# The graph layer's norm and linear part moved into the attention loop, and its scatters six to an iteration

## The chip, the cores and the metric

The kernel runs on one core of a Trainium2 chip. The metric is the time of one execution on the device in microseconds. Four engines compute: TensorE (PE, matrix products and transposes into PSUM banks), VectorE (DVE), ScalarE (ACT) and GpSimd (POOL). POOL also issues the indirect DMAs, whose addresses are rows of an index tensor; SyncE (SP) issues the plain ones. Engines run their own instruction streams and wait for each other on semaphores.

## The reference

Two layers act on 64 x 256 = 16384 tokens of width 64. The change lies between the local attention and the feed-forward part of layer 1. Its attention (`_L1_attn_ref`) works in windows of 64 tokens with 8 heads, and its feed-forward part is gated by a graph layer over 262144 edges:

```python
h = h + _L1_attn_ref(_layernorm(h), ...)
h = h + _L1_ffn_ref(_layernorm(h), ...)

# in _L1_ffn_ref, x = _layernorm(h), M = 16384 nodes, 4 heads x 4 experts
h = (x_flat @ W_gat).reshape(M, HEADS, NUM_EXPERTS)
a_src = (h * att_src).sum(-1)
a_dst = (h * att_dst).sum(-1)
e = leaky_relu(a_src[src] + a_dst[dst], 0.2)
e_max = segment_max(e, dst); ee = exp(e - e_max[dst])
alpha = ee / (segment_sum(ee, dst)[dst] + 1e-16)
agg = segment_sum(h[src] * alpha[:, :, None], dst) + b_gat
scores = _layernorm(agg, ln_gamma, ln_beta).reshape(M, HEADS, NUM_EXPERTS).mean(1)
topk_s, topk_i = top_k(scores, TOP_K); w = softmax(topk_s)
for ei in range(NUM_EXPERTS):
    g = where(topk_i == ei, w, 0.0).sum(-1)
    hh = gelu(x @ W1[ei] + b1[ei])
    out = out + g[..., None] * (hh @ W2[ei] + b2[ei])
```

## The kernel before

The 16384 rows are 128 tiles of 128. The residual `H` (in the rows: h_res) and the normed `xn` lie in SBUF for all tiles. The edges have been sorted by destination earlier, and while FFN0 (layer 0's experts) runs, POOL looks up for each node where its edges begin and end.

*Attention loop.* `Fori(0,AI=32)` on PE (L624) and ACT (from L828); DVE's loop is written out in Python (from L1230). An iteration handles four tiles, one in each of four lanes `AL`, with two PSUM banks per lane: `ps[0]` are banks 0, 2, 4, 6 and `ps[1]` banks 1, 3, 5, 7. The steps are listed in `A_STEPS`: PE does xT, qkv, sc, PT, pv, oT, pj; ACT does xs, xTs, q (L835), ex (L837), PTs (L838), oTs (L839), with xs being L831 and xTs L833; DVE does kb (L1238), vb (L1241), mx (L1243), sb (L1244), sm (L1245), rc (L1246), on (L1247), h (L1250). Each step is one instruction or a few for each lane, all four lanes before the next step, and `need` makes an engine wait for named steps of the others. All products go through the helper `mm` (L398), so rows of PE all have that line. Ahead of an iteration's steps DVE calls `prepare(i)`, which finishes the edge search in pieces: comparisons at i = 4 to 7, end positions at 8, operations over 128x2048 at 25 to 30, the rest at 31, where it raises `s_gi`.

*norm(2)*, L1102 to L1109 on DVE and L792 to L798 on ACT: mean, squares, deviation and product over all tiles in two halves.

*Linear part.* `Fori(0,GI=16)` with two lanes `GL` of four tiles. ACT copies `xn` (L848), PE transposes it (xT), ACT copies the transpose (L851, `xTs`), PE multiplies by `gw` (hg), ACT copies the 16 values of each node into `nodeG` (L854), DVE forms the source and destination terms (L1262 and L1263, twice). SP stores the transposes (L292, read back by ffn1) and the node rows (L294). POOL scatters the destination terms, one indirect DMA per tile, to the first edge of each node (L378).

*Gather stage.* POOL then gathers the node row of each edge's source, 32 chunks of 64 gathers (L386), in three buffers. With each of the first eight chunks go two iterations of ffn1, the expert products (PE L672, ACT L867, DVE L1276, loads by SP L301). DVE scans the chunk's edges, SP stores the sums, and 128 gathers of segment ends (L394) and the gating close the program.

## Time and profile before

| | us |
|---|---|
| median of 3 runs | 6204.32 (6192.32 to 6206.57) |
| profiled execution | 6180.4 |
| its span | 6178.7 |
| attention loop | 1998 to 2573 |
| norm(2) | 2573 to 2616 |
| linear part | 2616 to 2842 |
| ffn1 and gathers | 2842 to 3924 |
| gathers and scans | 3924 to 5882 |
| ends and gating | 5882 to 6178 |

Times of rows count from the span's start. The profiled execution is 24 us shorter than the median of the three runs, so it is compared with another profiled span, and the median with a median. Over the span PE is busy 42%, DVE 37%, ACT 19% and POOL 43%, with a mean granted TensorE clock of 0.658 of full speed. In the listing of steps "x4" or "x8" counts records; one fp32 `mm` call leaves two matmul records.

### The profile page before, as it was taken

What the parts mean: (1) busy time and instruction counts of PE and PEld (TensorE: products, weight loads), DVE (VectorE), ACT (ScalarE), POOL (GpSimd) and SP (SyncE); (2) the same over time, 40 slices, a digit from 0 to 9 for tenths busy, and PEclk for the clock granted to TensorE, in tenths of its full rate; (3) what the DMA queues carried; (4) which work ended last, traced back from release to release, by engine and by line L of the source; (5) the groups of instructions that cost most, each with busy time, mean ns of one, the idle gap of its engine ahead of it and who ended that gap; (6) DMA issues with size and microseconds to landing.
All of it is one profiled execution on the core that took longest, in us unless ns stands there. A gap on an engine that the chain in (4) does not pass through costs nothing.

```text
span 6178.7 us, 71504 instructions
## 1 busy us (share of the span) xinstructions
PE 2596.5 (42%) x28363; PEld 1934.5 (31%) x28363; DVE 2308.1 (37%) x4906; ACT 1185.0 (19%) x2669; POOL 2665.5 (43%) x2593
## 2 busy tenths in 40 slices
PE   5777878757986888643145455100000000000000
PEld 5777777744222767542033333000000000000000
DVE  7866566666345776710011121211111110111136
ACT  2333333323343554410011111000000000000000
POOL 0000000002545000056735545677777777777753
PEclk9888989877787999855555555555555555555555
DMA  0022322223673130012111111111111111111113
GB/s 29 9 36 39 44 32 34 27 45 73 156 159 100 1 28 0 3 26 50 13 36 43 30 41 38 29 20 20 16 17 19 19 14 19 19 19 14 19 46 106
DMA packets 317481, 229.93 MB, mean 37 GB/s; under 512 B 178077, under 2 KB 264910, under 8 KB 314894
## 3 DMA queue, kind: packets, MB, share of 16 engines
q1 hardware_dynamic: 213582, 179.40, 13.8%
q0 software_dynamic: 82016, 33.49, 5.3%
q10 hardware_dynamic: 21632, 13.63, 0.9%
q8 instruction: 164, 2.69, 0.2%
q14 instruction: 87, 0.71, 0.0%
HBM read 153.62 MB, written 72.71 MB: 37 GB/s over the span
## 4 chain that ended last, share of the span: by engine, by line
issue 34%; PE 27%; DVE 17%; another core or an unknown queue 15%; ACT 3%; DMA 3%; SPq 0%; POOL 0%; DVEq 0%; ACTq 0%; POOLq 0%
PE bank L398 26%; DVE arena L970 1%; DVE arena L1238 1%; DVE arena L1243 1%; DMA arena<-sort_exchange 1%; DVE arena L1303 1%; DMA arena<-gate_rows 1%; DVE arena L969 1%; ACT arena L867 1%; DVE arena L975 1%; DVE arena L974 1%; DVE arena L1392 1%; DVE arena L1103 0%; DVE ln_stat L1102 0%
## 5 line engine op out<-in xcount | busy, mean ns | idle before, releaser
L398 PE MATMUL bank<-arena 64*64 64x64 f32 (+12 forms) x26246 | 2312.6, 289 | 1096.4 <-ACT arena L867 397.3
L386 POOL DMA_INDIRECT arena<-node_table,arena x2048 | 2120.4, 1035 | 919.8 <-issue 629.6
L398 PEld LDWEIGHTS bank<-arena 64*64 64x64 f32 (+5 forms) x26246 | 1673.1, 166 | 1721.9 <-issue 945.9
L688 PE MATMUL bank<-ident,arena 128*20 128x128 f32 x3 | 0.8, 409 | 1994.5 <-remote 1994.5
L688 PEld LDWEIGHTS bank<-ident,arena 128*20 128x20 f32 x3 | 0.3, 111 | 1994.8 <-remote 1994.7
L363 POOL MEMSET arena<- 128x512 f32 x1 | 0.5, 529 | 1353.3 <-DVE h_res L1041 1353.3
L1288 DVE COPY arena<-arena 128x4 f32<-128x4 f32 x32 | 5.5, 172 | 1317.6 <-DMA arena<-node_table,arena 1317.3
L378 POOL DMA_INDIRECT edge_dst_terms<-arena,start_idx x128 | 125.9, 983 | 719.3 <-DVE arena L1263 679.7
L869 ACT ACTIVATE arena<-arena 128x512 f32<-128x512 f32 x32 | 20.1, 629 | 2019.1 <-issue 1482.3
L1276 DVE TENSOR_TENSOR arena<-bank,arena 128x512 f32<-128x512 f32 x64 | 43.6, 690 | 959.1 <-remote 818.7
L398 PE MATMUL bank<-ident,arena 128*128 128x128 f32 (+2 forms) x2048 | 291.6, 315 | 180.5 <-ACT arena L837 81.5
L398 PEld LDWEIGHTS bank<-ident,arena 128*128 128x128 f32 (+2 forms) x2048 | 259.1, 187 | 215.5 <-DVE arena L1244 107.9
L867 ACT ACTIVATE arena<-bank,arena 128x512 f32<-128x512 f32 x128 | 83.5, 687 | 912.2 <-remote 713.1
L1177 DVE TENSOR_TENSOR arena<-arena 128x512 f32<-128x512 f32 x256 | 170.0, 690 | 181.7 <-PE bank L398 88.4
L1303 DVE TENSOR_TENSOR_SCAN arena<-arena 128x64 f32<-128x64 f32 x640 | 196.8, 375 | 109.1 <-issue 107.9
L367 POOL DMA_INDIRECT arena<-row_pivots,pivot_row_idx x128 | 133.8, 1045 | 218.4 <-DVE pivot_row_idx L1149 111.8
L814 ACT ACTIVATE arena<-bank,arena 128x512 f32<-128x512 f32 x256 | 161.0, 689 | 261.5 <-PE bank L398 234.8
L372 POOL DMA_INDIRECT arena<-sorted_keys,key_block_idx x128 | 141.7, 1107 | 140.7 <-DVE arena L1177 78.2
L969 DVE TENSOR_TENSOR arena<-arena 128x1024 f32<-128x1024 f32 x116 | 141.8, 1223 | 78.0 <-DMA arena<-sort_exchange 75.5
L394 POOL DMA_INDIRECT arena<-sums_sorted,end_idx x128 | 135.0, 1054 | 40.1 <-issue 38.7
L970 DVE TENSOR_TENSOR arena<-arena 128x1024 f32<-128x1024 f32 x116 | 141.4, 1219 | 0.0
L837 ACT ACTIVATE arena<-arena 128x512 f32<-128x512 f32 x128 | 77.5, 630 | 161.5 <-DVE arena L1244 161.5
(350 smaller groups left out, 2607.5 us busy)
## 6 DMA issues: line engine op xcount, KB each, us to landing
arena<-gate_rows SPq DMA_DIRECT2D x256, 256.0 KB
arena<-node_table,arena POOLq DMA_INDIRECT x2048
sums_sorted<-arena SPq DMA_DIRECT2D x32, 768.0 KB
expert_out<-arena SPq DMA_DIRECT2D x64, 256.0 KB
arena<-expert_out SPq DMA_DIRECT2D x16, 1024.0 KB
sort_exchange<-arena SPq DMA_DIRECT2D x14, 1024.0 KB, 4.3
arena<-in_x_dram ACTq DMA_DIRECT2D x36, 256.0 KB, 3.7
edge_dst_terms<-arena SPq DMA_DIRECT2D x1, 4096.0 KB, 21.2
```

What stands on the lines that cost most here:

```text
L367: G.indirect_dma_start(out=land2[:,t,:],out_offset=None,in_=piv_d,in_offset=bass.IndirectOffsetOnAxis(ap=idx1[:,t:t+1],axis=0)).then_inc(s ...
L372: G.indirect_dma_start(out=land3[:,t,:],out_offset=None,in_=keysb,in_offset=bass.IndirectOffsetOnAxis(ap=idx2[:,c*(NT//2)+t:c*(NT//2)+t+1] ...
L378: G.indirect_dma_start(out=ad_e,out_offset=bass.IndirectOffsetOnAxis(ap=sidx[:,t:t+1],axis=0), in_=nodeG[:,t,20:24],in_offset=None,bounds_ ...
L386: G.indirect_dma_start(out=rch[:,j%NB,c,:],out_offset=None,in_=tbl, in_offset=bass.IndirectOffsetOnAxis(ap=gidx[:,j*CW+c:j*CW+c+1],axis=0) ...
L394: G.indirect_dma_start(out=ends[:,t,:],out_offset=None,in_=sums_d,in_offset=bass.IndirectOffsetOnAxis(ap=eidx[:,t:t+1],axis=0)).then_inc(s ...
L398: mm=lambda o,a,b,st=True,sp_=True: nc.tensor.matmul(o,a,b,start=st,stop=sp_,skip_group_check=True)
L814: A.activation(B.hT[:,n%3,:],B.ps[n%3][:,:],ACT.Gelu,bias=fb1[:,n%8:n%8+1]).then_inc(B.ge,1)
L867: A.activation(B.hT[:,u%2,:],B.ps[u%2][:,:],ACT.Gelu,bias=lb1[:,u:u+1]).then_inc(B.act,1)
L969: V.tensor_tensor(y[:,:,0,:],x[:,:,0,:],x[:,:,1,:],ALU.min)
L970: lk(V.tensor_tensor(y[:,:,1,:],x[:,:,0,:],x[:,:,1,:],ALU.max))
L1177: V.tensor_tensor(B.hS[:,x%2,:],B.hT[:,x%3,:],GB[:,l,x%3,:],ALU.mult).then_inc(B.mu,1)
L1303: last=V.tensor_tensor_scan(R[:,:,f],xe[:,0,:,head(f)],R[:,:,f],carry[:,1-b,f:f+1],ALU.mult,ALU.add)
```

## The change

The norm, transposes, products and terms of eight tiles are done inside the attention loop once their h is final, two iterations behind. With j = i//2-1, an even iteration i (from 2) carries the norm of tiles 8j to 8j+7 and their transposes, an odd one (from 3) the products and terms. The last eight tiles follow after the loop. norm(2) and the loops over `GL` are gone. PE's and ACT's attention loops are written out in Python as DVE's was. `prepare` now runs at i = 0 to 11 and raises `s_gi` there. POOL scatters six tiles per iteration from i = 12, each six behind the last h of that iteration, and the last eight when their terms are ready. SP's zero fill of the scatters' target moves ahead of its wait for the end positions; it stores x and node rows once per eight tiles. The transposes are read from `xn` without a copy.

```diff
+FINAL=11
...
-        GL=lanes("gat",2,4,first=1); take=bump(C0+8192,D0)
-        for B in GL:
-            B.xs=take([4,D]); B.xT=take([512]); B.tm=take([4,16])
+        xsq=take([8,D]); xTg=take([8*P]); tmg=take([8,16])
...
+            sp.wait_ge(s_zf,1)
+            sp.dma_start(ad_e.rearrange("(p a b) f -> p a (b f)",p=P,a=16),zfill.unsqueeze(1).broadcast_to((P,16,512))).then_inc(s_zs,16)
-            sp.wait_ge(s_zf,1)
-            sp.dma_start(ad_e.rearrange("(p a b) f -> p a (b f)",p=P,a=16),zfill.unsqueeze(1).broadcast_to((P,16,512))).then_inc(s_zs,16)
-            with sp.Fori(0,GI) as i:
-                for l in range(2):
-                    need(sp,GL[l],G_STEPS,i,"act:xTs")
-                    sp.dma_start(x4[:,bass.ds(i*2+l,1),:],GL[l].xT[0:D].unsqueeze(1)).then_inc(s_xst[l],16)
-                    need(sp,GL[l],G_STEPS,i,"dve:rd")
-                    sp.dma_start(t4[:,bass.ds((i*2+l)*4,4),:],nodeG[:,bass.ds((i*2+l)*4,4),:]).then_inc(s_tst[l],16)
-            ended(sp,GL,G_STEPS,GI)
-            for l in range(2): sp.wait_ge(s_xst[l],16*GI); sp.wait_ge(s_tst[l],16*GI)
+            for j in range(GI):
+                sp.wait_ge(s_gxs,j+1)
+                sp.dma_start(x4[:,2*j:2*j+2,:],xTg[0:D].rearrange("p (n t) -> p n t",n=2)).then_inc(s_xst,16)
+                sp.wait_ge(s_gtm,j+1)
+                sp.dma_start(t4[:,8*j:8*j+8,:],nodeG[:,8*j:8*j+8,:]).then_inc(s_tst,16)
+            sp.wait_ge(s_xst,16*GI); sp.wait_ge(s_tst,16*GI)
...
-            for i in range(GI):
-                for l in range(2):
-                    need(pool,GL[l],G_STEPS,i,"dve:rd")
-                    for t in range((i*2+l)*4,(i*2+l)*4+4):
-                        G.indirect_dma_start(out=ad_e,out_offset=bass.IndirectOffsetOnAxis(ap=sidx[:,t:t+1],axis=0),
-                            in_=nodeG[:,t,20:24],in_offset=None,bounds_check=NE-1,oob_is_err=False).then_inc(s_ads,16)
-            ended(pool,GL,G_STEPS,GI)
-            for l in range(2): pool.wait_ge(s_tst[l],16*GI)
+            SC0=FINAL+1
+            for t in range(NT):
+                pool.wait_ge(s_gtm,t//8+1)
+                if t%6==0 and SC0+t//6<AI: need(pool,AL[3],A_STEPS,SC0+t//6,"dve:h")
+                G.indirect_dma_start(out=ad_e,out_offset=bass.IndirectOffsetOnAxis(ap=sidx[:,t:t+1],axis=0),
+                    in_=nodeG[:,t,20:24],in_offset=None,bounds_check=NE-1,oob_is_err=False).then_inc(s_ads,16)
+            for B in AL: need(pool,B,A_STEPS,AI-1,"dve:h","act:oTs","pe:pj")
+            pool.wait_ge(s_tst,16*GI); pool.wait_ge(s_xst,16*GI); pool.wait_ge(s_gn,GI); pool.wait_ge(s_gx,GI)
...
             for B in FL: pe.wait_ge(B.ha,NK); pe.wait_ge(B.ge,LAST); pe.wait_ge(B.mu,LAST)
             pe.wait_ge(s_w2,16*8)
-            with pe.Fori(0,AI) as i:
+            def turned(j):
+                pe.wait_ge(s_gn,j+1)
+                for l,B in enumerate(AL):
+                    for t in range(8*j+2*l,8*j+2*l+2): r=mm(B.ps[1][0:D,(t%2)*P:(t%2+1)*P],xn[:,t,:],ident[:,:])
+                r.then_inc(s_gx,1)
+            def products(j):
...
+                r.then_inc(s_gh,1)
+            for i in range(AI):
...
+                if i%2 and i>=3: products(i//2-1)
+                if i%2==0 and i>=4: pe.wait_ge(s_ghs,i//2-1)
+                if i%2 and i>=3: pe.wait_ge(s_ghs,i//2); pe.wait_ge(s_gxs,i//2)
...
+                if i%2==0 and i>=2: turned(i//2-1)
-            with pe.Fori(0,GI) as i:
-                def step(fn,*names):
-                    for B in GL:
-                        need(pe,B,G_STEPS,i,*names)
-                        fn(B).then_inc(B.pe,1)
-                def xT(B):
-                    for t in range(4): r=mm(B.ps[0][0:D,t*P:(t+1)*P],B.xs[:,t,:],ident[:,:])
-                    return r
-                step(xT,"act:xs")
-                def hg(B):
-                    for t in range(4): r=mm(B.ps[1][:,t*16:(t+1)*16],B.xT[0:D,t*P:(t+1)*P],gw[0:D])
-                    return r
-                step(hg,"act:xTs")
...
-            with act.Fori(0,AI) as i:
+            def deviation(j):
+                act.wait_ge(s_gc,j+1)
+                A.activation(xsq,xn[:,8*j:8*j+8,:],ACT.Square).then_inc(s_gq,1)
+                A.preload_act_table_set("natural_log")
+                act.wait_ge(s_gv,j+1)
+                A.activation(lst[:,2,8*j:8*j+8],lst[:,1,8*j:8*j+8],ACT.Ln,scale=1.0/D,bias=eps[:,0:1]).then_inc(s_gl,1)
+                act.wait_ge(s_gl,j+1)
+                A.activation(lst[:,3,8*j:8*j+8],lst[:,2,8*j:8*j+8],ACT.Exp,scale=-0.5).then_inc(s_gr,1)
+            def turned(j):
+                act.wait_ge(s_gx,j+1)
+                if j: act.wait_ge(s_xst,16*j)
+                for l,B in enumerate(AL): r=A.copy(xTg[0:D,2*l*P:2*(l+1)*P],B.ps[1][0:D,0:2*P])
+                r.then_inc(s_gxs,1)
+            def products(j):
+                act.wait_ge(s_gh,j+1)
+                A.copy(nodeG[:,8*j:8*j+8,0:16],AL[3].ps[1][:,2*P:3*P].rearrange("p (t f) -> p t f",t=8)).then_inc(s_ghs,1)
+            for i in range(AI):
...
+                if i%2==0 and i>=2: deviation(i//2-1)
+                if i%2 and i>=3: products(i//2-1)
+                if i%2==0 and i>=2: turned(i//2-1)
-            norm_act(2)
-            act.wait_ge(s_xn,6)
-            def gat(i,first):
-                def step(fn,*names):
-                    for l,B in enumerate(GL):
-                        need(act,B,G_STEPS,i,*names)
-                        fn(B,l).then_inc(B.act,1)
-                step(lambda B,l:A.copy(B.xs,xn[:,bass.ds((i*2+l)*4,4),:]))
-                def xTs(B,l):
-                    if not first: act.wait_ge(s_xst[l],16*i)
-                    return A.copy(B.xT[0:D],B.ps[0][0:D,:])
-                step(xTs,"pe:xT")
-                def hgs(B,l):
-                    return A.copy(nodeG[:,bass.ds((i*2+l)*4,4),0:16],B.ps[1][:,0:D].rearrange("p (t f) -> p t f",t=4))
-                step(hgs,"pe:hg")
-            gat(0,True)
-            with act.Fori(1,GI) as i:
-                gat(i,False)
-            ended(act,GL,G_STEPS,GI)
+            deviation(GI-1); turned(GI-1); products(GI-1)
+            act.wait_ge(s_gtm,GI)
...
-                if i==4: dve.wait_ge(s_l3,16*NT)
-                if 4<=i<8: below(NT//2+16*(i-4),16,64,land3[:,16*(i-4):16*(i-4)+16,:],land3[:,16*(i-4):16*(i-4)+16,:],r3)
+                if i==0: dve.wait_ge(s_l3,16*NT)
+                if i<4: below(NT//2+16*i,16,64,land3[:,16*i:16*i+16,:],land3[:,16*i:16*i+16,:],r3)
-                if i==31:
+                if i==FINAL:
...
+            row8=lambda r,j: lst[:,r,8*j:8*j+8].unsqueeze(2).broadcast_to((P,8,D))
+            def centred(j):
+                h=H[:,8*j:8*j+8,:]
+                for B in AL: need(dve,B,A_STEPS,2*j+1,"dve:h")
+                lk(V.tensor_reduce(lst[:,0,8*j:8*j+8],h,AX.X,ALU.add))
+                V.scalar_tensor_tensor(out=xn[:,8*j:8*j+8,:],in0=row8(0,j),scalar=-1.0/D,in1=h,op0=ALU.mult,op1=ALU.add).then_inc(s_gc,1)
+            def deviation(j):
+                dve.wait_ge(s_gq,j+1)
+                V.tensor_reduce(lst[:,1,8*j:8*j+8],xsq,AX.X,ALU.add).then_inc(s_gv,1)
+            def normed(j):
+                dve.wait_ge(s_gr,j+1)
+                V.tensor_tensor(xn[:,8*j:8*j+8,:],xn[:,8*j:8*j+8,:],row8(3,j),ALU.mult).then_inc(s_gn,1)
+            def terms(j):
+                dve.wait_ge(s_ghs,j+1)
+                for k in range(2):
+                    V.tensor_tensor(tmg,nodeG[:,8*j:8*j+8,0:16],gatt[:,k,:].unsqueeze(1).broadcast_to((P,8,16)),ALU.mult).then_inc(s_gp,1)
+                    dve.wait_ge(s_gp,2*j+k+1)
+                    last=V.tensor_reduce(nodeG[:,8*j:8*j+8,16+4*k:20+4*k],tmg.rearrange("p t (g e) -> p t g e",g=4),AX.X,ALU.add)
+                    if k==0: lk(last)
+                last.then_inc(s_gtm,1)
+                if i%2==0 and i>=2: centred(i//2-1)
...
+                if i%2==0 and i>=2: deviation(i//2-1)
+                if i%2==0 and i>=2: normed(i//2-1)
+                if i%2 and i>=3: terms(i//2-1)
...
-            norm(2)
-            for B in GL: V.memset(B.tm,0.0).then_inc(B.dve,1)
-            with dve.Fori(0,GI) as i:
-                def step(fn,*names):
-                    for l,B in enumerate(GL):
-                        need(dve,B,G_STEPS,i,*names)
-                        if not names[1:]: dve.wait_ge(B.dve,i*len(G_STEPS["dve"])+1)
-                        fn(B,l).then_inc(B.dve,1)
-                for k,(m,r_) in enumerate((("hgs","ms"),("hgs","md"))):
-                    step(lambda B,l:V.tensor_tensor(B.tm,nodeG[:,bass.ds((i*2+l)*4,4),0:16],b4(gatt[:,k,:]),ALU.mult),"act:hgs",*(["dve:rs"] if k else []))
-                    step(lambda B,l:V.tensor_reduce(nodeG[:,bass.ds((i*2+l)*4,4),16+4*k:20+4*k],B.tm.rearrange("p t (g e) -> p t g e",g=4),AX.X,ALU.add),f"dve:{r_}")
-            ended(dve,GL,G_STEPS,GI)
+            centred(GI-1); deviation(GI-1); normed(GI-1); terms(GI-1)
+            dve.wait_ge(s_gtm,GI)
```

What stands in a row on the engines, first PE between the values (pv, 64x16) and the output projection in any iteration, before:

```order
L398 MATMUL bank4<-arena 64x16 x8
L398 MATMUL bank6<-arena 64x16 x8
L210 REGISTER_ALU
L398 MATMUL bank0<-ident,arena 64x128
L398 MATMUL bank2<-ident,arena 64x128
L398 MATMUL bank4<-ident,arena 64x128
L398 MATMUL bank6<-ident,arena 64x128
```

The output's transposes (bank0 to bank6, 64x128) follow the values directly. After, in an even iteration:

```order
L396 MATMUL bank4<-arena 64x16 x8
L396 MATMUL bank6<-arena 64x16 x8
L396 MATMUL bank1<-ident,arena 64x128 x2
L396 MATMUL bank3<-ident,arena 64x128 x2
L396 MATMUL bank5<-ident,arena 64x128 x2
L396 MATMUL bank7<-ident,arena 64x128 x2
L396 MATMUL bank0<-ident,arena 64x128
L396 MATMUL bank2<-ident,arena 64x128
L396 MATMUL bank4<-ident,arena 64x128
L396 MATMUL bank6<-ident,arena 64x128
```

Eight transposes of the graph layer, two in each lane's second bank, stand between pv and oT. After, in an odd iteration between qkv and the scores:

```order
L396 MATMUL bank4<-arena 64x64 x8
L396 MATMUL bank6<-arena 64x64 x8
L396 MATMUL bank7<-arena 128x16 x8
L396 MATMUL bank1<-arena 128x512
L396 MATMUL bank3<-arena 128x512
```

The row with bank7 and 128x16 is the eight products. On ACT between q and the next iteration's first copies, before:

```order
L835 COPY arena<-bank4 64x64 x2
L835 COPY arena<-bank6 64x64 x2
L210 ISA
L837 ACTIVATE arena<-arena 128x512 x4
L210 REGISTER_ALU
L838 COPY arena<-bank1 128x512
L838 COPY arena<-bank3 128x512
L838 COPY arena<-bank5 128x512
L838 COPY arena<-bank7 128x512
L210 REGISTER_ALU
L839 COPY arena<-bank0 64x128
```

The exponential (L837) follows q (L835). After, in an even iteration, first around the exponential (L859):

```order
L855 COPY arena<-bank4 64x64 x2
L855 COPY arena<-bank6 64x64 x2
L829 ACTIVATE arena<-arena 128x512
L830 ACT_TABLE_LOAD
L832 ACTIVATE ln_stat<-ln_stat,eps 128x8
L834 ACT_TABLE_LOAD
L834 ACTIVATE ln_stat<-ln_stat 128x8
L859 ACTIVATE arena<-arena 128x512 x4
```

and then from the copies of the output's transposes (L861) to the next iteration's first copies (L851):

```order
L861 COPY arena<-bank6 64x128
L839 COPY arena<-bank1 64x256
L839 COPY arena<-bank3 64x256
L839 COPY arena<-bank5 64x256
L839 COPY arena<-bank7 64x256
L851 COPY arena<-arena 128x64 x4
```

Square, Ln and Exp of the norm with two table loads come ahead of the exponential, and four copies of the transposes ahead of the next iteration. On DVE between vb (L1241) and rc, before:

```order
L1241 TENSOR_TENSOR arena<-bank6,arena 128x128
L1243 TENSOR_REDUCE arena<-bank1 128x8
L1243 TENSOR_REDUCE arena<-bank3 128x8
L1243 TENSOR_REDUCE arena<-bank5 128x8
L1243 TENSOR_REDUCE arena<-bank7 128x8
L1244 TENSOR_TENSOR arena<-bank1,arena 128x512
L1244 TENSOR_TENSOR arena<-bank3,arena 128x512
L1244 TENSOR_TENSOR arena<-bank5,arena 128x512
L1244 TENSOR_TENSOR arena<-bank7,arena 128x512
L1245 TENSOR_REDUCE arena<-arena 128x8 x4
```

Maxima (L1243) follow vb, and the sums (L1245) follow the subtractions (L1244). After, the same place in an even iteration:

```order
L1271 TENSOR_TENSOR arena<-bank6,arena 128x128
L1247 TENSOR_REDUCE ln_stat<-arena 128x8
L1274 TENSOR_REDUCE arena<-bank1 128x8
L1274 TENSOR_REDUCE arena<-bank3 128x8
L1274 TENSOR_REDUCE arena<-bank5 128x8
L1274 TENSOR_REDUCE arena<-bank7 128x8
L1275 TENSOR_TENSOR arena<-bank1,arena 128x512
L1275 TENSOR_TENSOR arena<-bank3,arena 128x512
L1275 TENSOR_TENSOR arena<-bank5,arena 128x512
L1275 TENSOR_TENSOR arena<-bank7,arena 128x512
L1251 TENSOR_TENSOR arena<-arena,ln_stat 128x512
L1278 TENSOR_REDUCE arena<-arena 128x8 x4
```

The reduction of the squares (L1247) stands ahead of the maxima (L1274) and the multiplication by the deviation (L1251) behind the subtractions (L1275).

## Rows read from the trace of the kernel before

**Rows 1.** The page, section 2: busy tenths of POOL in 40 slices of 154.5 us.

```profile
POOL 0000000002545000056735545677777777777753
```

**Rows 2.** By stage: us, busy (x instructions) per engine, clock, DMA share, GB/s.

```profile
1998.00:2573.00 575.00, 490.75 (x6120) 400.76 (x6117) 422.67 (x1060) 283.28 (x888) 0.00 (x0) 0.96 0.14 8
...
2616.00:2842.00 226.00, 114.72 (x507) 101.60 (x508) 27.72 (x133) 37.67 (x96) 126.65 (x129) 0.56 0.16 27
```

**Rows 3.** The same view: two attention iterations, then the end of FFN0.

```profile
2299.80:2317.00 17.20, 14.68 (x193) 11.93 (x194) 12.51 (x33) 8.86 (x29) 0.00 (x0) 1.00 0.00 0
...
2317.00:2335.80 18.80, 16.28 (x193) 13.53 (x194) 12.49 (x32) 8.94 (x29) 0.00 (x0) 0.91 0.00 0
...
1473.00:1713.00 240.00, 211.59 (x664) 61.09 (x664) 90.86 (x144) 90.00 (x146) 133.34 (x128) 0.82 0.69 154
```

**Rows 4.** Timeline of DVE, one iteration: start, us, line, operands, [idle before <-releaser].

```profile
2215.84 2.48 DVE L1238 TENSOR_TENSOR arena<-bank,arena 128x512 f32<-128x512 f32 x4 [1.89 <-ACT arena L835]
...
2219.04 2.47 DVE L1243 TENSOR_REDUCE arena<-bank 128x8 f32<-128x512 f32 x4
...
2223.82 2.45 DVE L1245 TENSOR_REDUCE arena<-arena 128x8 f32<-128x512 f32 x4
...
2227.59 0.23 DVE L1247 TENSOR_TENSOR arena<-bank,arena 128x64 f32<-128x64 f32 x1 [1.01 <-PE bank L398]
```

**Rows 5.** Timeline of ACT, the same iteration.

```profile
2222.14 2.42 ACT L837 ACTIVATE arena<-arena 128x512 f32<-128x512 f32 x4 [4.92 <-DVE arena L1244]
...
2229.21 0.95 ACT L839 COPY arena<-bank 64x128 f32<-64x128 f32 x4 [1.86 <-PE bank L398]
...
2230.35 0.68 ACT L831 COPY arena<-arena 128x64 f32 x4 [0.19 <-issue]
```

**Rows 6.** Timeline of PE, the same iteration (windows from 2213.5 and from 2217).

```profile
2213.62 1.09 PE L398 MATMUL bank<-ident,arena 128*64 128x128 f32 x8
...
2216.68 3.70 PE L398 MATMUL bank<-arena 128*128 128x512 f32 x8
```

**Rows 7.** Groups by form: xcount | busy us, mean ns | idle before, releasers.

```profile
L398 PE MATMUL bank<-arena 64*128 64x16 f32 x256 | 52.1, 342 | 81.6 <-ACT arena L851 58.0 <-issue 23.5
...
L724 ACT ACTIVATE arena<-bank 128x256 f32<-128x256 f32 x32 | 12.3, 385 | 103.1 <-PE bank L398 103.1
...
L796 ACT ACT_TABLE_LOAD x6 | 7.7, 1283 | 0.1
```

**Rows 8.** Timelines at the handovers: last h, last terms, first ffn1 matmul, first gather.

```profile
2572.91 0.22 DVE L1250 TENSOR_TENSOR h_res<-h_res,bank 128x64 f32<-128x64 f32 x1
...
2823.21 0.43 DVE L1263 TENSOR_REDUCE arena<-arena 128x64 f32 x2
...
2829.95 15.34 PE L398 MATMUL bank<-arena 64*128 64x512 f32 x31 [8.38 <-DMA arena<-xT_d]
...
2842.51 0.97 POOL L386 DMA_INDIRECT arena<-node_table,arena  x1 [0.31 <-issue]
```

**Rows 9.** Timelines of POOL, SP and ACT around one burst of sixteen scatters.

```profile
2647.51 0.98 POOL L378 DMA_INDIRECT edge_dst_terms<-arena,start_idx  x1 [8.23 <-DVE arena L1263]
...
2666.82 0.98 POOL L378 DMA_INDIRECT edge_dst_terms<-arena,start_idx  x1 [0.30 <-issue]
...
2655.44 0.73 SPq L294 DMA_DIRECT2D node_table<-arena  x1
...
2675.27 0.40 SPq L294 DMA_DIRECT2D node_table<-arena  x1
...
2662.78 0.58 ACT L851 COPY arena<-bank 64x512 f32<-64x512 f32 x1 [8.26 <-remote]
```

**Rows 10.** Timelines of POOL and DVE in norm(1), and the group of L1177.

```profile
1983.73 5.20 POOL L372 DMA_INDIRECT arena<-sorted_keys,key_block_idx  x1 [0.30 <-issue]
...
1983.70 8.75 DVE L1109 TENSOR_TENSOR arena<-arena,ln_stat 128x4096 f32<-128x4096 f32 x2
...
L1177 DVE TENSOR_TENSOR arena<-arena 128x512 f32<-128x512 f32 x256 | 170.0, 690 | 181.7 <-PE bank L398 88.4 <-DMA arena<-gate_rows 58.0 <-issue 14.4
```

26 lines of the change are left out of this document (15 added, 11 removed).

## The prediction

> **What bounds the kernel now.** I read the slices of the page first, then busy time by stage, then single iterations as timelines, and last the places where one stage hands over to the next. The slices of POOL [rows 1] show two parts. Up to slice 18 it works only in places and the other engines set the time. From 2842 us on it issues gathers nearly without a pause until the last slice, and nothing overtakes it: the end of the program lies a fixed stretch of gathers behind the first gather. Whatever lets the first gather and the first load of ffn1 start earlier should move the end by as much, as long as that stage keeps its pace.
>
> Three stretches stand ahead of the first gather [rows 2]. In the attention loop (1998 to 2573) PE is busy 490.75 of 575 us at a clock of 0.96. In the linear part of the graph layer (2616 to 2842) PE is busy 114.72 of 226 us and DVE 27.72: nothing is full there, and the time is waits from engine to engine. Between them lies the norm over all tiles. The handovers [rows 8] give the size of what can be had: the loop's last addition to h starts at 2572.91, the last terms end at 2823.21 + 0.43 = 2823.6, ffn1's first matmul starts at 2829.95 and the first gather at 2842.51. The change takes away the stretch from 2572.9 to 2823.6, **250.7 us**, and puts its work into the loop and a short tail. The question is what the loop then costs.
>
> **What an iteration has room for.** An iteration takes 17.20 us at full clock, and 18.80 when TensorE falls to its lower level (1.2 for 2.4 GHz) for a moment in it [rows 3]; the mean is 575/32 = 18.0. The path through it goes from engine to engine: PE makes q, k, v, DVE builds the key blocks (L1238), PE the scores, DVE maximum and subtraction, ACT the exponential, PE its transposes, ACT copies them, PE the values, DVE the scaling, PE and ACT the transposed output. DVE idles 1.89 us before L1238 and 1.01 us before L1247 [rows 4]. ACT idles 4.92 us before its exponential and 1.86 us before L839 [rows 5]. A piece that is put in front of one of these idle stretches is free up to its length; one on the path costs its whole duration.
>
> **Even iterations (eight tiles' norm and transposes).**
> - DVE at the start: a reduction and a scalar_tensor_tensor of 128x512. Four reductions of that size take 2.45 us [rows 4], so some 0.62 to 0.69 each, 1.3 together, under the 1.89 us of idle: 0. If that cover were gone it would cost its 1.3.
> - ACT after q: Square of 128x512 (0.6, as the exponential's 2.42 for four [rows 5]), two table loads of 1283 ns [rows 7], two tiny activations: some 3.7 us under 4.92 us of idle: 0, with 1.2 us left.
> - DVE reduction of the squares between L1241 and the maximum: DVE works there without a gap, so +0.7.
> - DVE multiplication by the deviation after the subtraction: 0.69 under 1.01: 0.
> - PE: eight transposes of 64x128 between the values and the output's transposes. One step of four takes 1.09 us [rows 6], so +2.1. All four scalings are through by then, so it replaces no wait.
> - ACT: four copies 64x256 ahead of the next iteration's L831 copies. 128x256 from a bank takes 385 ns [rows 7], so 1.5 us. In the trace L831 starts 0.2 us after L839 ends [rows 5], and PE's next transposes wait for it, with no slack: +1.5. Sum of an even iteration: **+4.3** (bounds 3.0, if half the transposes and copies overlap, to 6).
>
> **Odd iterations (products and terms).**
> - PE: eight products 128x16 before the scores. The form takes 342 ns at the lower clock [rows 7], pipelined about 1.06 us for eight records; the sixteen here take 1.3 to 2.1 us. The scores run from 2216.68 over 3.70 us and DVE gets to the first maximum at about 2219.1, so the first lanes have room and the last has none: +1.15 (bounds 0 and 2.1).
> - ACT copy of 0.25 us in idle time: 0.
> - DVE terms: two multiplications and two reductions of 128x128. The 128x64 ones take 0.2 each [rows 8]; 1.35 us against 1.01 of idle: +0.35. Sum: **+1.5** (0.3 to 2.5).
>
> A pair of iterations costs 5.8 us, and fifteen pairs **87 us** (50 to 125).
>
> **Other entries in the loop.** The edge search's rest moves from iterations 4 to 31 to 0 to 11. It is the same DVE work and was uncovered before too, so it nets out, but iteration 0 now waits for the last lookups POOL issued (+3) and at iterations 2, 6, 8 and 10 the search and the centring stand before L1238 together (+1.3 each, 5). A longer loop at the same habits of the clock has more dips, and less dense PE work may bring a few more: +12 (a dip costs 1.6 us [rows 3]; 7 more; bounds 2 and 40). SP's zero fill is issued ahead of the wait for the end positions, now before the loop; its queue carries nothing else then: 0. SP's stores, one of x and one of the table for eight tiles, land 20 us or more before their buffers are needed again: 0. For six scatters in each of iterations 12 to 31, I put 5 us of friction (0 to 110, below). The loop grows by 87 + 3 + 5 + 12 + 5 = **112 us**.
>
> **The tail.** The last eight tiles go through alone: centring 1.3, Square 0.6, tables and activations 3.1, two reductions' worth of DVE 1.4, transposes 2.1 and copies 1.5, products 2.1 and copy 0.3, terms 1.35, and some eight handovers of 0.1 to 0.2 us: **15 us** (13 to 18).
>
> So the terms are ready at 2572.9 + 112 + 15 = 2700 instead of 2823.6: **124 us earlier**. Behind that, ffn1's first matmul stood 6.3 us after the last terms and still does. The first gather stood 18.9 us behind; now eight scatters and the first node's row remain, 9 x 1.29 = 11.6, so gathers begin up to 7 us earlier yet, which counts only if the first chunk waits for gathers and not for ffn1. I leave it out of the sum and in the range. Iteration structure, chunk order and buffers of the gather stage are untouched, so everything behind shifts as a block. The profiled execution (6180.4 us, its span 6178.7) would come to 6056. The median of the three runs is 6204.3, 24 us above it; against the median I get **6080 us**.
>
> **Rivals.**
> *The bursts drag the loop.* While POOL issues indirect DMAs back to back, the other engines slow down after a while. A burst of sixteen scatters runs from 2647.51 to 2666.82 [rows 9]. SP's DMA instruction at 2655.44, 7.9 us into the burst, takes 0.73 us, and ACT's copy at 2662.78 came only after 8.26 us of idle. Six scatters are 6 x 1.29 = 7.7 us: they end 0.2 us before the drag showed. If they reach it, or if the count and not the time decides, an iteration loses 3.5 to 5.5 us, since each of its some ten handovers would take half a microsecond longer. Over twenty iterations that is 70 to 110 us: **6165 us** (6150 to 6190). It eats the whole gain from 124/20 = 6.2 us per iteration on. Against it: SP's instruction of the same line at 2675.27, 7.5 us after that burst, takes 0.40, and here each burst has some 12 us of rest.
> A lock between DVE and POOL would bring the same: an indirect DMA took 5.20 us while DVE had a multiplication with two SBUF inputs of 4.4 us running [rows 10], not 0.98 as a scatter's. In even iterations the centring's second instruction (0.69) falls into the burst and would stretch it to 8.4 us, past the 7.9. The Trainium skill ("SBUF — State Buffer", section "Who interferes with whom") says that a DVE instruction with two SBUF inputs and a GpSimd instruction that reads SBUF exclude each other for their whole length, whichever came first. The long DMA agrees for POOL's side. For DVE's side the trace speaks against it: the multiplications of L1177, beside POOL's lookups, average 690 ns like any of that size [rows 10]. By the rule DVE would also wait up to 0.98 us for centring behind a scatter, ten times, 10 us more.
> *TensorE's clock falls* (the slower side). Full clock is what the loop lives on: 0.96 in it, against 0.56 in the linear stage, where PE is busy 51% [rows 2]. FFN0, at 88% busy, had only 0.82 [rows 3], so a busy PE does not secure it. PE's density goes from 0.85 to about 0.84. One iteration with a clock of 0.91, that is 3.4 us at the lower level, costs 1.6 us, so 0.47 us for each us low. The gain is gone when 124/0.47 = 264 us of the 687 are low; at 60% low, less the 12 us counted, the loop loses 180 more: **6250 us**. For it: the added waits on ACT in odd and even iterations leave PE idle a little longer. Against it: those are tenths of a microsecond, beside the (17.20 - 14.68) = 2.5 us that PE is not busy in an iteration now.
> *Written-out code.* PE's and ACT's loops become 32 copies. PE issues 6120 matmuls and 6117 weight loads in 575 us [rows 2]; no row shows written-out code at 21 instructions per us (FFN0's is, at 664 matmuls in 240 us [rows 3]). If a fetch held PE 1.5 us in each iteration: 48 us, **6130 us** (bounds 0 and 3 us, up to 6175). Against it: DVE's part of this loop is written out already and shows no unexplained gap [rows 4].
> *More is hidden than I count.* If PE's extra transposes and the copies overlap their neighbours, the pair costs 4 us, not 5.8, and the 7 us of earlier gathers count: 27 + 7 more: **6045 us** (6030 to 6055).
>
> **How the numbers follow.** Forecast 0.66 (own range 6055 to 6110), bursts 0.14, written-out code 0.06, more hidden 0.09, clock 0.05. The range of 8 in 10 runs from **6040** to **6165**: it leaves out a third of "more hidden", the upper half of the bursts and the clock, some 0.15. A measurement of this kernel can tell about 0.3% (18.6 us) from no change, so faster means below 6186 and slower above 6223. Faster: all but the worst bursts and the clock, 0.90. Same: 0.04. Slower: 0.06.
>
> **What would show it.** Even iterations should come at some 21.5 us and odd ones at 18.7 to 19 at full clock; the loop should end near 2686, the terms near 2700, ffn1's first matmul near 2707 and the first gather near 2712. DVE's idle before the key blocks should shrink from 1.89 to about 0.5 in even iterations, and the two table loads should lie inside ACT's wait for the exponential. Iterations 12 to 31 should be no longer than 2 to 11 but for the scatters' friction: if they are by 3 us or more, and instructions of all engines in the burst stand further apart, the first rival is right. A clock below 0.9 in the loop is the second's mark, gaps of PE that no other engine ends are the third's. The prediction is wrong if the stretch from the first gather to the end is not the same to a few microseconds, or if ffn1's first chunk takes the gain back.

## The result and the profile after

The changed kernel takes 6236.3 us in the median of 15 runs (6207.6 to 6259.0), the kernel before 6197.0 in 15 runs (6176.4 to 6216.1). The ratio is 1.0064 with a 95% interval of 1.0048 to 1.0080: 39 us slower, where 6080 us and a clear gain had been forecast. The profiled execution of the changed kernel has a span of 6257.3 us, 78.6 above the one of before. Some 30 us of that lie ahead of the attention loop, in code that the change doesn't touch: lane 3's first addition to h starts at 2046.6 here and at 2015.8 before, and the other kernels below, with the same code there, have it between 2018 and 2041. So differences are read inside the loop and behind it.

The first view is busy time by engine over the loop, from the first iteration's last h to the 32nd's: us, busy us and instructions of PE, its weight loads, DVE, ACT and POOL, granted clock, DMA share, GB/s. The second line of after is its iterations 13 to 31. Before:

```profile
2015.80:2572.90 557.10, 475.07 (x5952) 388.71 (x5952) 409.61 (x1028) 275.46 (x865) 0.00 (x0) 0.96 0.15 8
...
2230.90:2572.90 342.00, 293.16 (x3648) 240.58 (x3648) 248.86 (x633) 168.96 (x529) 0.00 (x0) 0.96 0.00 0
```

After:

```profile
2046.60:2893.60 847.00, 664.97 (x6432) 522.25 (x6431) 471.71 (x1146) 348.17 (x1014) 112.03 (x114) 0.80 0.12 8
...
2345.70:2893.60 547.90, 435.86 (x3952) 335.60 (x3952) 279.38 (x684) 213.27 (x625) 112.03 (x114) 0.78 0.05 8
```

The loop grew by 290 us, not by 112, and TensorE's mean granted clock in it fell from 0.96 to 0.80 of its 2.4 GHz (its levels are 1.2 and 2.4). From iteration 13 on, where scatters run, an iteration takes 547.9/19 = 28.8 us, against 342.0/19 = 18.0. Behind the loop everything is as forecast. The timelines of DVE and POOL there:

```profile
2894.39 0.69 DVE L1242 TENSOR_REDUCE ln_stat<-h_res 128x8 f32<-128x512 f32 x1 [0.56 <-DVE h_res L1283]
...
2910.36 0.29 DVE L1258 TENSOR_REDUCE arena<-arena 128x32 f32<-128x128 f32 x1
...
2923.01 0.97 POOL L384 DMA_INDIRECT arena<-node_table,arena  x1 [0.30 <-issue]
```

They answer to [rows 8]: the last h starts at 2893.6, the last terms end at 2910.65, 17 us later, and the first gather starts 12.4 us behind them. From the first gather to the end it is 6257.3 - 2923.0 = 3334.3 us, before 6178.7 - 2842.5 = 3336.2. The stage shifted as a block. The miss is all in the loop, and it has two places. One is a single iteration, in the timelines of SP and ACT:

```profile
2112.14 0.39 SPq L283 DMA_DIRECT2D end_positions<-end_pos  x1
2148.23 0.37 SPq L285 DMA_DIRECT2D start_pos<-end_positions  x1
2148.65 8.68 SPq L291 DMA_DIRECT2D xT_d<-arena  x1
```

```profile
2160.16 1.17 ACT L839 COPY arena<-bank 64x256 f32<-64x256 f32 x4 [29.96 <-DMA xT_d<-arena]
```

ACT stands 30 us ahead of its copy of the second eight tiles' transposes, for the store of the first eight's, because both use one buffer. That store is ready at iteration 2 but stands in SP's program behind the wait for the end positions, behind their store (2112.14 to 2148.2, 36 us) and behind the load of the start positions. Iteration 5 takes 55.8 us.

The other place repeats in each iteration that has scatters, in the timelines of POOL (six DMAs from 2550.62, 1.29 us apart) and of PE in the same burst:

```profile
2550.62 0.98 POOL L376 DMA_INDIRECT edge_dst_terms<-arena,start_idx  x1 [22.30 <-DVE h_res L1283]
```

```profile
2550.39 1.98 PE L396 MATMUL bank<-arena 65*64 65x64 f32 x52
2552.69 0.31 PE L396 MATMUL bank<-arena 65*64 65x64 f32 x3 [0.32 <-issue]
2553.43 0.49 PE L396 MATMUL bank<-arena 65*64 65x64 f32 x5 [0.44 <-issue]
2554.15 3.75 PE L396 MATMUL bank<-arena 65*64 65x64 f32 x8 [0.22 <-issue]
2560.54 3.59 PE L396 MATMUL bank<-arena 128*128 128x512 f32 x4 [2.64 <-DVE arena L1268]
```

PE makes q, k and v with 64 small matmuls and their weight loads, 16 for each lane. The first 52 leave at full pace. Then, 1.8 us after POOL's first scatter started, PE pauses with nothing to wait for ("issue") behind every three to five matmuls. These pauses are short, 1.0 us here. The row of eight that takes 3.75 us holds the last four small matmuls, through by 2554.7, and behind them four of the scores' 128x512 ones, which the view merges with them; the other four scores are the row of 2560.54.

The long wait of this iteration is on ACT, which copies q and k of each lane when PE is through with it. Its timeline in the same burst:

```profile
2551.24 0.42 ACT L855 COPY arena<-bank 64x64 f32<-64x64 f32 x2 [0.39 <-PE bank L396]
2554.20 0.42 ACT L855 COPY arena<-bank 64x64 f32<-64x64 f32 x2 [2.53 <-remote]
2559.25 0.87 ACT L855 COPY arena<-bank 64x64 f32<-64x64 f32 x4 [4.63 <-remote]
```

and the same eight copies in an even iteration of the kernel that has no scatters in the loop (the first experiment):

```profile
2599.61 1.82 ACT L856 COPY arena<-bank 64x64 f32<-64x64 f32 x8 [0.38 <-PE bank L397]
```

PE's records have the third lane's matmuls end at 2552.1, and PE had run four 128x512 matmuls behind them by 2557.9. Yet the update of the semaphore that ACT waits for is recorded at 2559.23 only, and ACT starts 0.02 us after it. ("Remote" is the view's word for an update that comes too long after any instruction's end to be matched with it.) The updates of the third and fourth lane's products and of two lanes' scores, whose matmuls end between 2552.1 and 2557.9, are all recorded between 2559.23 and 2559.47. So PE has done its work, and the news of it reaches ACT up to 7 us late.

### The profile page after: what moved, and what is told of

Its sections match the earlier page's. It is cut to its first block, busy times and chain, and to the rows that moved or that the text cites. A ratio compares the mean times of both kernels' runs of the same rounds, so it can differ in the third digit from the quotient of the medians.

```text
span 6257.3 us, 70198 instructions
## 1 busy us (share of the span) xinstructions
PE 2695.6 (43%) x28363; PEld 1974.4 (32%) x28363; DVE 2315.5 (37%) x4896; ACT 1213.5 (19%) x2723; POOL 2661.0 (43%) x2593
## 4 chain that ended last, share of the span: by engine, by line
issue 30%; PE 29%; DVE 15%; another core or an unknown queue 13%; POOL 5%; ACT 4%; DMA 4%; SPq 0%; DVEq 0%; ACTq 0%; POOLq 0%
PE bank L396 29%; POOL arena L384 5%; DVE arena L975 1%; DMA arena<-sort_exchange 1%; DVE arena L1326 1%; DVE arena L974 1%; DVE arena L980 1%; DMA arena<-gate_rows 1%; ACT arena L872 1%; DVE arena L979 1%; DVE arena L1274 1%; DVE arena L1415 1%; DMA end_positions<-end_pos 1%; DMA sort_exchange<-arena 0%
## 5 line engine op out<-in xcount | busy, mean ns | idle before, releaser
L396 PE MATMUL bank<-arena 64*64 64x64 f32 (+14 forms) x26246 | 2414.1, 292 | 1090.6 <-ACT arena L872 407.9
L396 PEld LDWEIGHTS bank<-arena 64*64 64x64 f32 (+5 forms) x26246 | 1710.3, 167 | 1771.7 <-issue 1036.7
L874 ACT ACTIVATE arena<-arena 128x512 f32<-128x512 f32 x32 | 20.1, 629 | 2020.9 <-issue 1037.2
L1299 DVE TENSOR_TENSOR arena<-bank,arena 128x512 f32<-128x512 f32 x64 | 43.6, 690 | 950.0 <-remote 796.3
L1268 DVE TENSOR_TENSOR arena<-bank,arena 128x512 f32<-128x512 f32 x128 | 83.5, 687 | 183.4 <-ACT arena L855 112.0
```

The source lines that it names most:

```text
L396: mm=lambda o,a,b,st=True,sp_=True: nc.tensor.matmul(o,a,b,start=st,stop=sp_,skip_group_check=True)
```

## The experiments

Each changed kernel's iterations 13 to 31 are given as the same view as above, so that the lines compare: 547.90 us at 0.78 for the changed kernel, 342.00 at 0.96 for the one before.

**All scatters behind the loop.** They wait for the last h:

```diff
-                if t%6==0 and SC0+t//6<AI: need(pool,AL[3],A_STEPS,SC0+t//6,"dve:h")
+                if t==0:
+                    for B in AL: need(pool,B,A_STEPS,AI-1,"dve:h")
```

> The changed kernel with all 128 scatters behind the last h of the attention loop; everything else of the change stays. Theory 1 (the scatters' bursts drag PE's instructions, and the pauses pull TensorE's clock down): iterations 13 to 31 shrink from 28.9 to the 22.6 us that iterations 2 to 12 have, 19 x 6.3 = 120 us, and the low clock in them from 13.7 to 5 us each; the 120 scatters that no longer hide add about 120 x 1.29 = 155 us behind the terms, so the whole is some 35 us slower than the changed kernel. Theory 2 (the longer iterations are the clock's own habit, or the written-out code's): they stay at 27 to 29 us and the whole is 150 us slower.

Measured: 6212.5 us (10 runs), ratio to the kernel before 1.0035 (1.0020 to 1.0050), so 24 us *faster* than the changed kernel by the medians, where the theory had it 35 us slower. Its iterations 13 to 31, and its loop:

```profile
2327.70:2724.80 397.10, 340.42 (x3952) 276.24 (x3952) 274.82 (x686) 211.41 (x625) 0.00 (x0) 0.93 0.06 11
...
2031.00:2724.80 693.80, 566.00 (x6432) 459.50 (x6432) 467.07 (x1148) 345.98 (x1014) 0.00 (x0) 0.90 0.14 9
```

An iteration takes 20.9 us. The scatters cost the loop 547.9 - 397.1 = **151 us**, 7.9 per iteration, a little more than the 7.7 that POOL needs for six. Of the 153 us that the whole loop gains, 141 are given back behind it, where the first gather now stands 170.3 us behind the last h and not 29.4. Hiding the scatters in the loop that way gained nothing. It also shows what the linear part itself costs: at full clock 19.4 us in even iterations, and 21.3 in odd ones with a 3.4 us dip of the clock in nearly each. That is 2.9 us over the 18.0 of before, as forecast (5.8 per pair). In PE's timeline of an odd iteration q, k, v and the products now run without a pause:

```profile
2578.02 4.08 PE L397 MATMUL bank<-arena 65*64 65x64 f32 x80
```

**Written-out loops alone.** The kernel before with `for i in range(AI)` in place of `Fori(0,AI)` on PE and ACT:

```diff
-            with pe.Fori(0,AI) as i:
+            for i in range(AI):
...
-            with act.Fori(0,AI) as i:
+            for i in range(AI):
```

> The kernel before, with only PE's and ACT's attention loops written out in Python. Theory 3 (written-out code is fetched too slowly, or lowers the clock): iterations grow from 17.9 by more than 1 us, the whole by more than 30 us. Theories 1 and 2: no change in the iteration, the whole within 10 us of the kernel before.

Measured: ratio 0.9990 (0.9974 to 1.0006), iterations 13 to 31 in

```profile
2254.70:2592.50 337.80, 290.45 (x3649) 237.62 (x3648) 249.01 (x634) 166.92 (x528) 0.00 (x0) 0.96 0.01 2
```

17.8 us each. Written-out code costs nothing here, at 11 matmuls and as many weight loads in a microsecond. Ahead of these iterations it does show once. In iteration 9, while the store of the end positions (issued at 2160.1) is in flight, PE stops inside q, k and v with nothing to wait for (the last eight of the 27 are scores):

```profile
2176.80 1.62 PE L398 MATMUL bank<-arena 65*64 65x64 f32 x45
2184.11 7.48 PE L398 MATMUL bank<-arena 65*64 65x64 f32 x27 [5.70 <-issue]
```

That iteration takes 27.3 us, against 19.5 in the kernel before. Such a pause of PE beside that store, 1.6 to 8.0 us long and ending 23 to 27 us behind its issue, stands in six profiles of kernels with a written-out loop, and in neither of the two with PE's loop kept. In the other four ACT's wait in iteration 5 leaves PE idle at that time.

**Scatters alone.** The kernel before, loops kept, with 120 scatters more into a table that nobody reads, six behind each h from iteration 11 on. This work is extra, so the whole must be slower; the iteration is what counts.

```diff
...
+            G.iota(scr_i[:,:],pattern=[[2048,NT]],base=0,channel_multiplier=16).then_inc(s_sci,1)
+            pool.wait_ge(s_sci,1)
+            for t in range(120):
+                if t%6==0: need(pool,AL[3],A_STEPS,11+t//6,"dve:h")
+                G.indirect_dma_start(out=scr_d,out_offset=bass.IndirectOffsetOnAxis(ap=scr_i[:,t:t+1],axis=0),
+                    in_=ones_f[:,20:24],in_offset=None,bounds_check=NE-1,oob_is_err=False).then_inc(s_scr,16)
+            pool.wait_ge(s_scr,16*120)
             pool.wait_ge(s_gi,1); pool.wait_ge(s_zs,16)
```

> The kernel before, plus 120 extra scatters of 128 rows of 16 bytes each into a scratch table, six behind the last h of each iteration from 11 on, so in iterations 12 to 31; PE and ACT stay loops and no linear part is moved. Theory A (the drag is of POOL's indirect DMAs on any dense row of PE's instructions): iterations 12 to 31 grow from 18.0 to 25 to 26 us, as the changed kernel's grew by 7.9. Theory B (only written-out code is dragged, since its instructions are fetched by DMA beside the scatters'): they stay at 18 to 19 us.

Measured: ratio 1.0227 (1.0203 to 1.0252). Iterations 13 to 31, and PE's timeline in one burst (POOL's first scatter at 2505.65):

```profile
2246.20:2724.30 478.10, 366.13 (x3648) 272.67 (x3648) 253.76 (x633) 169.58 (x529) 114.54 (x114) 0.82 0.01 1
```

```profile
2505.47 1.92 PE L406 MATMUL bank<-arena 65*64 65x64 f32 x52
2507.67 0.31 PE L406 MATMUL bank<-arena 65*64 65x64 f32 x3 [0.28 <-issue]
2508.39 0.45 PE L406 MATMUL bank<-arena 65*64 65x64 f32 x5 [0.41 <-issue]
2509.11 3.81 PE L406 MATMUL bank<-arena 65*64 65x64 f32 x8 [0.27 <-issue]
```

25.2 us in place of 18.0: 136 us over 19 iterations, with the same pauses at the same point of the same row, 1.7 us into the burst. The same was done to the written-out variant of the kernel before:

> The same 120 extra scatters in the kernel before with PE's and ACT's attention loops written out. Theory A: the same 25 to 26 us in iterations 12 to 31. Theory B: here 25 to 26, with the loops kept 18 to 19.

Measured: ratio 1.0220 (1.0190 to 1.0250), 25.0 us per iteration. So the drag needs neither the written-out code nor the moved linear part. It comes with POOL's indirect DMAs beside the making of q, k and v.

One iteration with the loop kept, number 27, has its six scatters at the head too and yet takes 17.6 us at full clock. A search step of DVE runs there beside the first scatter, which takes 2.35 us, so that the second one starts when the 64 small matmuls are over (timelines of DVE, POOL and PE):

```profile
2607.11 2.28 DVE L1220 TENSOR_TENSOR arena<-arena 128x2047 f32<-128x2047 int32 x1
...
2607.90 2.35 POOL L378 DMA_INDIRECT scratch_rows<-ones_f,scratch_idx  x1 [18.47 <-DVE h_res L1258]
2610.55 0.99 POOL L378 DMA_INDIRECT scratch_rows<-ones_f,scratch_idx  x1 [0.30 <-issue]
...
2607.72 2.20 PE L406 MATMUL bank<-arena 65*64 65x64 f32 x64
```

With the loop written out the same iteration takes 19.2 us. So six scatters cost next to nothing when five of them stand behind q, k and v.

**Where the time goes in an iteration.** This is read from the records of the traces, as means over iterations 13 to 31. The first column is the whole iteration. The second is the stretch from the first small matmul of q, k and v to the end of ACT's last copy of them. The last gives how long behind the end of a lane's last small matmul ACT's copy of it starts, lane by lane.

| | iteration, us | q, k, v to ACT's last copy | rest | ACT behind PE, lanes 0 to 3 |
|---|---|---|---|---|
| before | 18.0 | 2.7 | 15.3 | 0.04, 0.04, 0.04, 0.04 |
| before, with scatters | 25.2 | 9.0 | 16.2 | 0.2, 2.2, 5.6, 4.7 |
| changed, scatters behind the loop | 20.9 | 2.7 | 18.2 | 0.04, 0.04, 0.04, 0.04 |
| changed | 28.8 | 9.4 | 19.5 | 0.5, 3.4, 6.6, 3.8 |
| changed, bursts moved (below) | 22.5 | 2.8 | 19.7 | 0.04, 0.04, 0.04, 0.04 |

Of the 7.9 us that the scatters add to an iteration of the changed kernel 6.7 lie in this stretch, and 6.3 of the 7.2 that they add in the kernel before. PE's own pauses sum to 2.2 and 1.0 us. So it is mainly the late news from PE to ACT that lengthens the iteration.

**Bursts cut into pairs.**

```diff
-                if t%6==0 and SC0+t//6<AI: need(pool,AL[3],A_STEPS,SC0+t//6,"dve:h")
+                if t%2==0 and SC0+t//6+(t%6>0)<AI: need(pool,AL[3],A_STEPS,SC0+t//6+(t%6>0),{0:"dve:h",2:"dve:vb",4:"dve:sm"}[t%6])
```

> The changed kernel with the six scatters of an iteration in three pairs, behind h, vb and sm of lane 3, 2.6 us each. Theory 1a (the drag needs POOL to issue for longer than a pair takes, as PE's first pause comes 1.5 us into a burst but the long ones from 4 us on): iterations 13 to 31 fall from 28.9 to 23 to 24 us, the whole by about 100 us. Theory 1b (each scatter drags by its own, some 1 us, wherever it stands): iterations stay at 28 to 30 us, the whole within 20 us of the changed kernel.

Measured: 6151.5 us (6 runs), ratio 0.9940 (0.9920 to 0.9959).

```profile
2325.80:2795.40 469.60, 401.68 (x3952) 319.72 (x3952) 278.67 (x685) 212.09 (x624) 111.25 (x113) 0.83 0.06 10
```

24.7 us, between the two theories: 85 us gained on the changed kernel, and each iteration still pays 3.8 us for six scatters. One pair stands on q, k, v, one on the values and the output's transposes, and one beside the scores.

**Bursts moved, whole.** Six in a row, but behind vb, beside the scores, maxima and exponential:

```diff
-                if t%6==0 and SC0+t//6<AI: need(pool,AL[3],A_STEPS,SC0+t//6,"dve:h")
+                if t%6==0 and SC0+t//6<AI: need(pool,AL[3],A_STEPS,SC0+t//6,"dve:vb")
```

> The changed kernel with each burst of six behind vb of its iteration in place of behind the h before, so beside the scores, maxima, subtraction, exponential and sums, where PE issues few and long matmuls. Theory C (the cost is that PE's 80 small products of q, k, v stand in the burst): iterations 13 to 31 fall from 28.8 to 22 to 24 us and the whole by 90 to 130 us. Theory D (each scatter costs the loop its 1.3 us wherever it stands): they stay at 28 to 29 us.

Measured: 6116.6 us (4 runs), ratio 0.9887 (0.9869 to 0.9906), 120 us less than the changed kernel. Iterations 13 to 31, then POOL's first scatter of a burst and PE around it:

```profile
2314.60:2741.40 426.80, 364.77 (x3953) 296.82 (x3952) 275.62 (x686) 211.81 (x625) 111.81 (x114) 0.88 0.06 10
```

```profile
2520.06 0.98 POOL L376 DMA_INDIRECT edge_dst_terms<-arena,start_idx  x1 [16.38 <-DVE arena L1271]
```

```profile
2514.66 5.83 PE L396 MATMUL bank<-arena 65*64 65x64 f32 x72
2523.52 5.47 PE L396 MATMUL bank<-ident,arena 128*128 128x128 f32 x32 [3.03 <-ACT arena L859]
2528.92 2.28 PE L396 MATMUL bank<-arena 128*64 128x16 f32 x61
```

22.5 us per iteration: the scatters now cost 1.6 instead of 7.9. The burst is as long as before, 7.7 us; it begins when PE has its small matmuls behind it and waits for ACT's exponential for 3 us anyway, and it is over before the 61 small ones of the values. Neither the burst's length nor its count decides, but what the others issue and hand over beside it.

**SP's order.** The first tiles' stores ahead of the end positions, the second's behind their store and ahead of the wait for it:

```diff
-            sp.wait_ge(s_eps,1)
-            with nc.allow_non_contiguous_dma(reason="node order"):
-                sp.dma_start(ep_d[1:M+1].rearrange("(t q) -> q t",q=P),endp[:,:]).then_inc(s_ep,16)
-                sp.wait_ge(s_ep,32)
-                sp.dma_start(startp[:,:],ep_d[0:M].rearrange("(t q) -> q t",q=P)).then_inc(s_epl,16)
...
             for j in range(GI):
+                if j==1:
+                    sp.wait_ge(s_eps,1)
+                    with nc.allow_non_contiguous_dma(reason="node order"):
+                        sp.dma_start(ep_d[1:M+1].rearrange("(t q) -> q t",q=P),endp[:,:]).then_inc(s_ep,16)
+                if j==2:
+                    sp.wait_ge(s_ep,32)
+                    with nc.allow_non_contiguous_dma(reason="node order"):
+                        sp.dma_start(startp[:,:],ep_d[0:M].rearrange("(t q) -> q t",q=P)).then_inc(s_epl,16)
```

> The changed kernel, but SP issues the first eight tiles' stores before it waits for the end positions, the second eight's behind the store of the end positions without waiting for it, and the load of the start positions after those. Theory: the 56 us of iteration 5 are ACT's wait for the first x store, which stands in SP's queue behind the 36 us of the end positions' store; iteration 5 falls to about 23 us and the whole by 33 us, to about the kernel before. Rival: the x store's data cannot pass the 16384 small pieces of the end positions' store in the rings, so the wait only moves to iteration 7, with a gain under 10 us.

Measured: 6182.7 us (10 runs), ratio 0.9985 (0.9970 to 1.0001). Iteration 5 falls from 55.8 to 29.5 us, 26 of the 33 expected: it is still at a clock of 0.77, and PE's pause beside the end positions' store, 3.2 us here, now falls into it. The loop goes from 847.0 to 801.6 us. The remaining 19 us are spread over the other iterations in steps of the clock; I don't take them for an effect of the order.

**Pairs and order together.**

> Scatters in pairs and SP's changed order of stores together. If the two gains are independent (85 and 54 us by the medians alone), the whole is some 6100 us, 90 us below the kernel before and 135 below the changed one; if the smoother loop only shifts where the waits are, it is between 6130 and 6150.

Measured: 6121.9 us (4 runs), ratio 0.9892 (0.9869 to 0.9916): 30 us below the pairs alone. Iteration 5 falls from 58.1 to 26.4 us, and the loops of the two profiled executions differ by 20.5 us. The independent sum of 6100 was not reached, which fits that the order alone is worth some 30 us and not 54.

**Both repairs.** The burst behind vb and SP's order:

> The changed kernel with both repairs: the bursts of six behind vb (beside the scores) and SP's changed order of stores. The burst's place gave 120 us by the medians, the order 54 alone and 30 beside the pairs: 30 to 50 us below the kernel with the bursts moved alone, 6070 to 6085 us. If the order's gain lies only in iteration 5 (30 us), 6085.

Measured: **6078.9 us** (4 runs), ratio 0.9809 (0.9777 to 0.9842).

**Products out of the way too.** In odd iterations PE's products go behind the scores, into the half of lane 3's first bank that vb has read; ACT's copy goes behind the exponentials and DVE's terms behind the reciprocals:

```diff
...
-                step(qkv,"act:xTs")
-                if i%2 and i>=3: products(i//2-1)
                 if i%2==0 and i>=4: pe.wait_ge(s_ghs,i//2-1)
-                if i%2 and i>=3: pe.wait_ge(s_ghs,i//2); pe.wait_ge(s_gxs,i//2)
+                step(qkv,"act:xTs")
+                if i%2 and i>=3: pe.wait_ge(s_gxs,i//2)
                 step(lambda B: mm(B.ps[1][:,:],B.Q,B.K.rearrange("p h j -> p (h j)")),"act:q","dve:kb")
+                if i%2 and i>=3: need(pe,AL[3],A_STEPS,i,"dve:vb"); products(i//2-1)
...
```

> The same, and in odd iterations PE's eight products stand behind the scores, in the second half of lane 3's first bank, ACT's copy of them behind the exponentials and DVE's terms behind the reciprocals. The scores begin 2.3 us late in odd iterations with the products ahead of them, and PE idles 2.0 us behind the scores. If the products' step is what it costs: odd iterations fall by 1 to 2 us each and lose part of their low clock, some 20 to 40 us in all, 6035 to 6060. Rival: the terms behind the reciprocals, 1.3 us against the wait for the values, take it back; then within 10 us of the run before.

Measured: **6033.5 us** (4 runs), ratio 0.9739 (0.9707 to 0.9770), 45 us below the run before it and the fastest of all. Iterations 13 to 31:

```profile
2293.40:2689.80 396.40, 352.72 (x3952) 295.52 (x3952) 272.42 (x685) 212.05 (x625) 105.33 (x107) 0.91 0.06 11
```

20.9 us with 107 scatters in the 19 iterations (six in each up to the 29th; the last ones wait for terms that now come later), no more than without any and with the products ahead of the scores.

## Why the prediction was wrong

**What bounds the kernel** held. The gather stage followed as a block (3334 against 3336 us), so each microsecond of the loop counted in full.

**The linear part in the loop** held. The forecast had 107 us without the friction of the scatters. The kernel with the scatters behind the loop has 693.8 - 557.1 = 136.7 us, of which iteration 5, at 59.7 us against some 22.5 of its odd neighbours, is 37.2, so 99.5. In detail two errors cancel. Even iterations cost 2.2 us at full clock, not 4.3: 19.4 against 17.2. PE's extra transposes and ACT's copies overlap (the copies take 1.17 us, not 1.5). Odd ones cost more: the scores begin 3.1 us after L1268's first instruction (2582.46 against 2579.32) where they began 0.8 after it [rows 4, 6], so the products delay them by 2.3 us, not 1.15, and the clock dips in nearly each of them. Moving them away brought 45 us.

**The tail** held: 17 us against 15, and the first gather 12.4 us behind the terms against 11.6.

**The scatters: the step that failed.** "For six scatters in each of iterations 12 to 31, I put 5 us of friction (0 to 110, below)." It was 151 us, over the upper end. The onset of 7.9 us came from SP and ACT in the linear stage [rows 9], and it was carried over to the loop as if it were POOL's alone. It is not. In that burst of the kernel before, ACT's copies at 2651.48 and 2653.40, up to 5.9 us into it, still start within 0.4 us of the end of PE's matmuls, and only the one at 2662.78 comes 6.5 us behind them. Over the linear stage PE issues 507 matmuls in 226 us, in the loop 6120 in 575 [rows 2]. In the dense row of small matmuls it pauses 1.8 us into the burst, and the second lane's update is already late. The burst was put right on this row, since h frees POOL just when q, k and v begin. The first rival named the right kind of loss, late handovers, but its decisive condition (passing 7.9 us, or a count) was wrong: six in a row beside the scores cost 1.6 us an iteration and six at the head 7.9. Its price was wrong too: not half a microsecond at each of ten handovers, but 3.4, 6.6 and 3.8 us at three that overlap.

**The clock** fell too, but as a follower. The second rival took it for a danger of its own. The granted clock is 0.78 in iterations 13 to 31, 0.93 with the scatters gone, 0.88 with them moved, and 0.82 in the kernel before when only scatters were added. At the 0.47 us that a microsecond at the lower level costs [rows 3], the low time of 0.22 x 2 x 547.9 = 241 us against 0.07 x 2 x 397.1 = 56 us would be worth 87 of the 151 us. The table above does not bear that out. 6.7 of the 7.9 us per iteration, 127 of the 151, lie where ACT waits for PE's updates, and there PE is idle for a good part; the rest of the iteration adds 1.25 us, 24 in all, though it holds matmuls at the lower level (four of 128x512 in 3.59 us, eight in 3.70 before [rows 6]). How much the clock costs inside the first stretch no run here separates. In that rival's text two numbers are off: 182 us on top of 6080 give 6260 us and not 6250, and PE's density came out at 566.0/693.8 = 0.82 without the scatters, not 0.84.

**SP's stores: a wait overlooked.** "SP's stores [...] land 20 us or more before their buffers are needed again: 0." That is true of the DMA and not of the queue. The end positions moved from iteration 8 to 4, and the stores moved behind them in SP's program. The store of the first eight tiles was ready in iteration 2 and issued in 5. It cost 33 us once, against 0. The wait was costed on the engine that makes the data and not on the queue that the store shares. With 146 us too little for the scatters, 33 for this and 7 too much for the linear part, 172 of the 178 us by which the loop missed are placed; the rest lies in iterations 2 to 12, at 22.6 us each against 21.9 in the kernel with the scatters behind the loop, from whose loop they differ mostly in the clock's dips.

**The other rivals.** Written-out code: out as a cost in each iteration, 17.8 us against 18.0. As a single pause beside the end positions' store it exists, 5.7 us in the run with nothing else changed. More hidden than counted: true in even iterations alone. The lock between DVE and POOL: in the changed kernel the centring inside a burst takes 0.70 us like outside (L1243), and no scatter takes over 1.42 us against a median of 0.98:

```profile
L376 POOL DMA_INDIRECT edge_dst_terms<-arena,start_idx x128: 980/982/1423, 2346.8 to 2920.4; - x128
```

So the lock, which the Trainium skill ("SBUF — State Buffer", section "Who interferes with whom") puts between DVE's instructions with two SBUF inputs and POOL's reads, is not what cost the time here. PE and ACT have no part in it, and the late handovers are theirs. The lock does show on POOL's side with a longer instruction: the scatter of 2.35 us above, beside a DVE instruction of 128x2047 with both inputs in SBUF, and that iteration was a fast one.

With both faults out, the same design runs at 6078.9 us, and the forecast was 6080. That they agree this closely is partly luck. In the profiled executions the loop of that kernel is 694.1 - 557.1 = 137 us longer than before, where 112 was forecast, and from the first iteration's last h to the end it gains 105 us, not 124; by the medians it gains 117 on a kernel before that was 8 us faster in these runs than the 6204 from which the forecast started.
